# GpSimd: one short instruction behind every scatter, and a later end of the scatters

## The reference

```python
xn = _layernorm(x, axis=-1)
x = x + attention(xn, Wq, Wk, Wv, Wo, We) + experts(xn, gate_w, w1, b1, w2, b2)

# attention: 16 heads of 8 columns, per batch
ctx = X @ We.T
influence = jnp.einsum('bqe,bke->bqk', ctx, ctx)
scores = jnp.einsum('bhqd,bhkd->bhqk', Q, K) * SCALE + 0.1 * influence[:, None]
out = softmax(scores) @ V, heads joined, @ Wo.T

# experts: 8 experts with 512 hidden columns, the best 2 for every row
probs = softmax(x @ gate_w.T); topk_probs, topk_idx = top_k(probs, 2)
y = w2[e] @ gelu(w1[e] @ x + b1[e]) + b2[e]      # for both chosen e
out = sum(y * topk_probs)
```

## Time and profile before

| what | value |
|---|---|
| median of three runs | 713.75 us |
| span of the profiled execution, first to last instruction | 791.5 us |
| granted TensorE clock, mean of the span | 0.958 |
| TensorE busy | 671.2 us, 85% |
| VectorE busy | 619.4 us, 78% |
| ScalarE busy | 538.9 us, 68% |
| GpSimd busy | 467.2 us, 59% |

### The profile page before, as it was taken

One profiled execution on the slowest core, in us unless ns is written; L12 is line 12 of the kernel. 1 busy time (PEld: TensorE's weight loads), 2 busy tenths in 40 slices (PEclk: granted clock), 3 DMA queues, 4 the chain that ended last, 5 costly groups with the idle time before them and its releaser, 6 DMA issues.

```text
span 791.5 us, 24553 instructions
## 1 busy us (share of the span) xinstructions
PE 671.2 (85%) x7800; PEld 433.1 (55%) x7800; DVE 619.4 (78%) x1106; ACT 538.9 (68%) x1123; POOL 467.2 (59%) x542
## 2 busy tenths in 40 slices
PE   0477888989889896969999999996689989988886
PEld 0463344444444443559999999993244444444444
DVE  8989878878778785948888888885587888887871
ACT  2581566776667685858888888884466766766765
POOL 8650656666566555306555565656676676676671
PEclk9997899999999998999999999999699999999998
DMA  9779545665455653664555454443376666566632
GB/s 262 253 212 299 138 125 146 154 175 158 117 159 148 176 155 100 174 111 90 101 105 102 96 109 102 103 89 100 77 153 161 159 165 166 152 161 161 159 92 61
DMA packets 162947, 113.32 MB, mean 143 GB/s; under 512 B 72624, under 2 KB 150448, under 8 KB 162864
## 3 DMA queue, kind: packets, MB, share of 16 engines
q1 hardware_dynamic: 153632, 90.63, 46.2%
q0 software_dynamic: 8192, 16.86, 8.6%
q10 hardware_dynamic: 1040, 4.76, 1.6%
HBM read 55.42 MB, written 47.19 MB: 130 GB/s over the span
## 4 chain that ended last, share of the span: by engine, by line
PE 71%; DVE 7%; issue 7%; SPq 5%; ACT 4%; another core or an unknown queue 3%; DMA 1%; ACTq 0%; DVEq 0%
PE bank L1133 20%; PE bank L1111 13%; PE bank L1251 12%; PE mx L1240 12%; PE mx L1145 7%; ACT A L708 4%; DVE mx L956 2%; PE bank L1193 2%; PE bank L1031 2%; PE bank L1162 2%; DVE A L791 2%; PE bank L1155 1%; SPq L319 1%; SPq L318 1%
## 5 line engine op out<-in xcount | busy, mean ns | idle before, releaser
L708 ACT ACTIVATE A<-bank 128x512 f32<-128x512 f32 x502 | 279.1, 602 | 109.9 <-PE bank L1133 94.1
L956 DVE TENSOR_REDUCE mx<-mx 128x4 f16<-128x1024 f32 x256 | 303.7, 1208 | 56.3 <-PE mx L1145 26.8
L1133 PE MATMUL bank<-stack 113*128 113x256 f16 x1004 | 185.2, 283 | 51.2 <-issue 24.9
L565 POOL DMA_INDIRECT slots_x<-rows,pos x128 | 123.5, 965 | 91.3 <-PE bank L1133 68.0
L579 POOL TENSOR_SCALAR rows<-rows,slot_p 128x128 f32<-128x128 f32 x142 | 112.1, 798 | 103.4 <-DVE rows L1007 103.4
L609 POOL DMA_INDIRECT rows<-slots_y,pos x128 | 121.5, 950 | 73.4 <-PE bank L1133 54.6
L1133 PEld LDWEIGHTS bank<-stack 113*128 113x128 f16 x1004 | 66.9, 99 | 164.9 <-issue 85.7
L1111 PE MATMUL bank<-A,V 128*32 128x256 f32 x2048 | 142.2, 397 | 1.7 <-ACT A L708 1.6
L752 ACT ACTIVATE rows<-mx,b 128x256 f32<-128x256 f32 x284 | 111.8, 474 | 30.0 <-PE mx L1240 30.0
L1001 DVE TENSOR_TENSOR rows<-rows 128x512 f16<-128x512 f32 x142 | 101.2, 714 | 25.2 <-ACT rows L756 22.8
L1251 PE MATMUL bank<-w,rows 128*128 x1704 | 108.2, 220 | 4.4 <-DVE rows L1001 4.4
(11 more groups left out here) (142 smaller groups left out, 616.8 us busy)
## 6 DMA issues: line engine op xcount, KB each, us to landing
stack<-ctx_rest SPq DMA_DIRECT2D x64, 256.0 KB
stack<-qk_dram SPq DMA_DIRECT2D x128, 96.0 KB
slots_y<-rows SPq DMA_DIRECT2D x71, 128.0 KB, 2.0
qk_dram<-hi_qk SPq DMA_DIRECT2D x64, 128.0 KB
stack<-ctx_high SPq DMA_DIRECT2D x128, 64.0 KB
slots_x<-A ACTq DMA_DIRECT2D x1, 4644.0 KB, 20.2
w_stage<-in_w SPq DMA_DIRECT2D x8, 512.0 KB
qk_dram<-lo_qk SPq DMA_DIRECT2D x64, 64.0 KB
```

The lines of the kernel that those rows point to most:

```text
L565: pool.indirect_dma_start(slots_x, bass.IndirectOffsetOnAxis(pos[j][:, t:t + 1], 0), rows[:, t, :].bitcast(F32), None).then_inc(s_scat, 16)
L708: act.activation(A[:, n % NA, :, :].rearrange("p h s -> p (h s)"), scores(k, n)[:, :], ACT.Exp, scale=SCALE).then_inc(s_xp, 1)
L956: dve.tensor_reduce(mx[:, a, 8 * qt:8 * qt + 8].rearrange("q (i e w) -> q i e w", i=2, e=2)[:, :, g % 2], MX[u % 2][:, :].rearrange("q (i ...
L1133: mm = pe.matmul(scores(k, n)[:, i * S:(i + 1) * S], stack[0:SHIFT + 1, par, h, 1, c * P:(c + 1) * P], stack[0:SHIFT + 1, par, h, 0, :], s ...
```

## The change

Behind every scatter stands exactly one other GpSimd instruction. Either it is a quarter of a chunk's low parts, 256 columns in place of 512 (28 quarters in place of 14 halves), or it is a fill of 480 columns of a new buffer `unread`, which nothing reads (100 fills). A fill waits for the fill before it. The numbers `n_ex` are spread wider, so that the last scatter waits for 248 blocks in place of 238, and the threshold for a chunk's parts is earlier. The waits on `s_wlo` count quarters.

```diff
+SPACE = 480
...
+        unread = sb("unread", [P, SPACE], F32)
...
-                    sp.wait_ge(s_wlo, 2 * c + 2)
+                    sp.wait_ge(s_wlo, 4 * c + 4)
...
-            def low_half(c, h):
-
-                cols = slice((2 * c + h) * WCH // 2, (2 * c + h + 1) * WCH // 2)
+            def low_quarter(c, h):
+
+                cols = slice((4 * c + h) * WCH // 4, (4 * c + h + 1) * WCH // 4)
                 pool.wait_ge(s_wsc, c + 1)
-                pool.tensor_tensor(w12[:, 1, cols], w_stage[:, h * WCH // 2:(h + 1) * WCH // 2], w12[:, 0, cols], ALU.subtract).then_inc(s_wlo, 1)
+                pool.tensor_tensor(w12[:, 1, cols], w_stage[:, h * WCH // 4:(h + 1) * WCH // 4], w12[:, 0, cols], ALU.subtract).then_inc(s_wlo, 1)
...
-                    n_ex = 2 * START + 2 + n * (16 * HALF - 2 * START - 20) // (2 * NT - 1)
+                    n_ex = 2 * START + 2 + n * (16 * HALF - 2 * START - 10) // (2 * NT - 1)
...
-                    c_lo, h_lo = n_low // 2, n_low % 2
-                    if c_lo < NCH - 1 and n_ex >= 16 * (2 * c_lo + 2) + 8 + 3 * h_lo:
-                        low_half(c_lo, h_lo)
+                    c_lo, h_lo = n_low // 4, n_low % 4
+                    if c_lo < NCH - 1 and n_ex >= 16 * (2 * c_lo + 2) + 6 + h_lo:
+                        low_quarter(c_lo, h_lo)
                         n_low += 1
-            assert n_low == 2 * (NCH - 1)
+                    else:
+                        if n_apart:
+                            pool.wait_ge(s_apart, n_apart)
+                        pool.memset(unread[:, :], 0.0).then_inc(s_apart, 1)
+                        n_apart += 1
+            assert n_low == 4 * (NCH - 1)
```

More of the change, by code:

```diff
@@ L255, in build @@
         s_const, s_zero, s_post = sem("s_const"), sem("s_zero"), sem("s_post")
-        s_fill = sem("s_fill")
+        s_fill, s_apart = sem("s_fill"), sem("s_apart")
         s_hiw, s_low = sem("s_hiw"), sem("s_low")
@@ L544, in places @@
                 pool.wait_ge(s_place, j + 1)
-            def low_half(c, h):
-                cols = slice((2 * c + h) * WCH // 2, (2 * c + h + 1) * WCH // 2)
+            def low_quarter(c, h):
+                cols = slice((4 * c + h) * WCH // 4, (4 * c + h + 1) * WCH // 4)
                 pool.wait_ge(s_wsc, c + 1)
-                pool.tensor_tensor(w12[:, 1, cols], w_stage[:, h * WCH // 2:(h + 1) * WCH // 2], w12[:, 0, cols], ALU.subtract).then_inc(s_wlo, 1)
-            n_low = 0
+                pool.tensor_tensor(w12[:, 1, cols], w_stage[:, h * WCH // 4:(h + 1) * WCH // 4], w12[:, 0, cols], ALU.subtract).then_inc(s_wlo, 1)
+            n_low = n_apart = 0
             places(0, Tb)
@@ L1227, in attend @@
                     if k == HALF and phase[0] == 0 and u == 5:
-                        for sm, n in ((s_red, 8 * (HALF + 1)), (s_wlo, 2 * NCH)):
+                        for sm, n in ((s_red, 8 * (HALF + 1)), (s_wlo, 4 * NCH - 2)):
                             pe.wait_ge(sm, n)
```

## The result

The kernel after takes 735.91 us (median of four runs, 734.67 to 737.53), the kernel before 714.04 in the same comparison: a ratio of 1.0308, 95% interval 1.0283 to 1.0332, which is 21.9 us more. The profiled execution of the kernel after has a span of 732.9 us; its device time is 734.67, so 1.8 us lie outside the span. It is not long, as that of before was: span and median agree.

The account below looks back on a forecast made before the run. GpSimd's sequence, 223.6 us from the first scatter to the last landing, was to overtake the attention blocks' 209.7 us in the first half; 713.75 + 14 = 728 us, own range 717 to 734, widest 705 to 736.

Parts of the forecast that it names:

- the widest range: Whole kernel: 705 to 736 us, meant to leave out no more than 0.2 of the chance.
- the rival of 741: First half: quarters at their upper price, blocks need 199 us and GpSimd 226, giving 741 us; chance 0.09.
- the blocks' way: Attention blocks from first scatter to transposing loads: 244.7 us in the profile, scaled to 209.7 us for a timed run.
- I take 36: First half of the attention: a timed run is 36 us shorter than the profiled 252, about 216 us.
- The even split: At least 67 us of the profile's excess shared equally by the two halves: 33.5 us each, 39 if the start gives nothing.
- GpSimd's list: GpSimd's sequence of scatters, fills and quarters from the first scatter to the last one landed: 223.6 us.
- The change of choice: GpSimd between first and second choice: waits for the landing and copies, adding 1.8 us beyond the hidden fill.
- nothing comes back: After the first half: TensorE's own work doesn't shrink, so all 14 us of lateness stay, 728 us.
- The price of a fill: GpSimd's fill of 480 columns: 0.50 us from two fills in the trace, bounds 0.40 and 1.10.
- The first rival: First half: runs of scatters stall the attention and the change ends that, so faster, around 706 us; chance 0.20.
- The second rival: GpSimd's slots: 0.17 and 0.02 us gaps due to recording, GpSimd needs 199 us, no change, 714 us; chance 0.14.
- the three waits of the earlier trace: On the chain before: waits of 3.96, 3.65 and 4.63 us, said to have every other engine resting, cause unnamed.

Follow-up runs that it names:

- the second profile of before: The kernel before, nothing edited, profiled once more: span 712.8 us, device time 714.51 us.

## Why the prediction was right in kind and short in size

- **The mechanism was right.** The time, 735.91 us, lies 1.9 us over the forecast's own 717 to 734; that it is still inside the widest range, by 0.1 us, is luck, for 736 was chosen only to leave out the rival of 741, in which GpSimd leads by more. The loss is 21.9 us where 14 were forecast. GpSimd's own list became the limit of the first half. No two scatters are 0.30 us apart; SyncE waits for low parts and, at the end, for the last landing; the time follows the length of the fills above a knee, and not below it.
- **The step that failed is the size of the blocks' way, "I take 36".** The prediction scaled 244.7 us of the long profile to 209.7, taking 35.0 off. In an ordinary execution the way is 203.9: 40.8 were to be taken off. The even split was nearly true (the second half had 255.0 us from the end of the experts in the first profile, 215.4 in the second), but the start gave nothing up, so the 39 us named as the other end were the nearer choice. That is 5.8 us of the 9.6 by which the lead was short (23.5 on the way where 14 was forecast).
- **GpSimd's list was 3.8 us short**, 223.6 against 227.4. Fills came as costed: 1.65 us a slot on the mean where 1.67 was said, 1.9 us less over 96 of them. Quarters took 0.681 us in place of 0.63, a slot 1.85 on the mean in place of 1.80: +1.5. The change of choice took 5.06 us from scatter to scatter where a slot and 1.8 were said: +1.6. The landing at the end took 1.34 us and not 1.85: -0.5. And one slot of 4.76 us, that of the 113th scatter, had no term in the sum at all: +3.1. Together +3.8.
- **The sum, mended**: 227.4 - 203.9 = 23.5 us on the way, less the 3.3 behind it and 0.1 ahead: 20.1, the difference of the two spans. The prediction had "nothing comes back"; in these two profiles the 3.3 us do, without a known cause. The rest to the 21.9 of the medians lies within the spread of the runs.
- **The price of a fill.** The row of the same operation was nearer (0.50 us, measured 0.515) than the estimate worked out from the Trainium skill (GPSIMD Engine Reference, sections 3.1 and 1), 0.41 us. Here 32, 240 and 480 columns take 142, 315 and 515 ns: 0.83 ns for each column and about 115 ns besides. By the 1.03 cycles of the Trainium skill (GPSIMD Engine Reference, section 3.1) a column takes 0.86 ns at the 1.2 GHz of its section 1, an estimate that is near the measured slope. "In place of 15" in the prediction's sentence on this price should be 14, by its own sum, and its 6 then 5.
- **The later end and the quarters cost nothing**: right within 1.7 us, by the interval of the kernel without fills.
- **The first rival, that runs of scatters stall the attention, falls.** The kernel with 32 columns has no runs and gains nothing, and the second profile of before has the runs without the long execution.
- **The second rival, a timed slot shorter than the profiled one, falls** too: the profiled execution of the kernel after took 734.67 us and its other runs 735.00 to 737.53, and two fills cost 56.1 us of time where the slots of the profile make 55.
- **Two misreadings.** One lies in the first paragraph of the prediction: that no engine bounds the first half was true only of that long execution. In the second profile TensorE is busy for 98.5% of the way. And the profiled span fell, as was said to be possible, but only because the profile of before had been long; GpSimd's waits for blocks were not the 20 us expected but next to none. The other is that in the three waits of the earlier trace rows "every other engine rests": in their 3.96, 3.65 and 4.63 us TensorE is busy for 2.55, 1.57 and 0.00, and GpSimd for 2.01, 2.03 and 3.21.
- **How the lateness went**, part in the batches and part at the end, was right. In the kernel after TensorE stands idle for 227.37 - 207.38 = 20.0 us of the way, 17.0 more than before, and is busy for 6.5 us longer: 23.5. Of the 6.5 some 2 are 24 matmuls more that lie inside the cut (an estimate, at the mean of 200.92 us for 2281); the rest goes with a granted clock of 0.96 in place of 1.00.

## What to carry to other kernels

An engine that runs a list beside the critical path has a budget: the other path's length less its own. Here it was some 13 us: 203.9 against a list of about 191 without fills (227.4 less 98 times 0.37, the 1.64 of a slot with a fill over the 1.27 of one without). The fills, 36 us, overdrew it by 23. The same 191 us with the fills of the other kernels gives 208 with 240 columns (the way there was 207.9), 282 with two fills (280.6), and 210 with fills in the first choice (210.5). What is inside the budget is free, and what is over it comes back about one for one. A wait of the list spends the budget too: with fills in the second choice the some 8 us that GpSimd waits before them have to be added, 191 + 18 + 8 = 217 (216.5). Work out that budget from a profiled execution whose span agrees with the timed median; where the only profile is long, take another one before splitting its excess by guess.

## What the runs showed of the hardware that was not expected

- **The stop ahead of the 114th scatter.** In every kernel here GpSimd's 114th indirect DMA starts late, however many fills stand before it, and whether it is held for block 212, as in the kernel before, or for block 221, as in those after. From the kernel after, and from that with two fills:

```profile
288.13 0.96 POOL L567 DMA_INDIRECT slots_x<-rows,pos  x1 [0.17 <-PE bank L1140]
289.09 0.51 POOL L577 MEMSET unread<- 128x480 f32 x1
292.89 0.97 POOL L567 DMA_INDIRECT slots_x<-rows,pos  x1 [3.29 <-PE bank L1140]
```

```profile
334.81 0.97 POOL L567 DMA_INDIRECT slots_x<-rows,pos  x1 [0.16 <-PE bank L1141]
335.77 1.07 POOL L578 MEMSET unread<- 128x480 f32 x2
340.63 0.98 POOL L567 DMA_INDIRECT slots_x<-rows,pos  x1 [3.79 <-PE bank L1141]
```

  The block named in brackets is not the cause: in the first trace TensorE has begun 460 matmuls of L1140 by 289.09 us, two for each block, so over 221 blocks were done. In the second profile of the kernel before the gap is 5.94 us. What it is stays open; no run was made for it.

- **The granted clock was lower where TensorE waited more.** Over the way the granted share of the full 2.4 GHz is 1.00 where TensorE is idle for 3.0 us (before), 0.96 with 20.0 us (after) and 0.88 with 64.0 us (two fills); its matmuls there take 200.92 us (2281 of them), 207.38 (2305) and 216.61 (2310). The third from its windows:

```profile
91.84:372.43 280.59, 216.61 (x2310) 116.77 (x2307) 193.70 (x314) 176.06 (x340) 247.99 (x362) 0.88 0.50 131
```

  In the kernel after, TensorE's longest wait on the way, 6.2 us, ends at 315.68 us; from 316 to 326 the grant is 0.50, the lower level of 1.2 GHz:

```profile
306.00:316.00 10.00, 3.83 (x44) 1.97 (x46) 5.80 (x11) 4.58 (x9) 8.97 (x12) 0.85 0.72 183
316.00:326.00 10.00, 7.17 (x39) 4.25 (x31) 1.20 (x3) 2.43 (x5) 2.20 (x4) 0.50 0.38 75
```

- **One profiled execution can be 78.7 us longer than the next of the same kernel**, 40.8 of it on the way and 39.6 in the second half (the rest, the start most of all, was 1.7 shorter), with no experiment that says why; the waits of the earlier trace rows belong to it.
